# A cross-attention and feed-forward kernel: the 4-byte matmuls of a pair of heads in one group, and the first blocks re-ordered

## The chip, the cores and the metric

The kernel runs on one core of a Trainium2 chip. The metric is the device time of one execution in microseconds. TensorE (PE) does the matmuls, VectorE (DVE), ScalarE (ACT) and GpSimd (POOL) the elementwise work, and SyncE (SP) issues every DMA.

## The reference

There are 16 sequences of 64 tokens (T = 1024 tokens), width 512, 32 heads of 128. Cut to what matters:

```python
q = layernorm(x) @ Wq;  k = ctx @ Wk;  v = ctx @ Wv        # 1024 x 4096 each
score = q @ k.T / sqrt(128) + position_bias                # by sequence and head, 64 x 64
probs = softmax(where(mask, score, -inf))
x = x + (probs @ v) @ Wo
y = layernorm(x)
x = x + y @ base_W.T + base_b + 2 * lora(y)                # router of 8 experts, rank 16
```

All is float32. The large products are made of fp32r parts ("hi" and "lo"), three matmuls for each; the scores, the transpositions and the products with v are plain 4-byte matmuls.

## The kernel before

**Blocks.** v, k and q are made in 48 blocks of two heads (or of 128+128 tokens for v): blocks 0 to 15 are v, 16 to 31 k, 32 to 47 q (`QA` = 32). A block is a 2x2 product by Strassen's way in Winograd's form: seven products p of half size, each of 6 matmuls of 512 columns (`times(n, p)`, line 1253 inside `product`). Products 1, 6, 5, 3 of a block add up in one PSUM bank, 2, 7, 4 in another. Between them ACT copies the bank out (`copy_p1` after 1, `copy_u` after 6, `copy_v` after 5, `copy_c12` after 3), and DVE makes the quarters `c11` (after 2), `c22` (after 7), `c21` (after 4). Product 6 waits for `c1_made` (the copy after 1), 7 for `c11_made`, 5 for `u_made`, 3 for `v_made`, 4 for `c22_made`. Block 0 is made by the plain eight products, so that it can start before sums of its operand exist.

**Weights.** A block of k or q has its own weight set w of seven slots: three are parts of the loaded `wk_raw`, four are sums that POOL makes (`sums_of_b`, tile `twk`). ACT casts a slot to "hi" (`higher(w, slot)`) once the product of the block before that used it is done, DVE subtracts for "lo" (`lower_w`). v has four sets, each for four blocks.

**Pairs.** A pair i of heads 2i, 2i+1 needs q (block 32+i, one tile q, written over in each block), and k and v, which earlier blocks stored in HBM (`load_k`, `load_v`, single buffers). For each head h: `scores(h)` (32 matmuls of 64 columns into bank `pS`), DVE adds the bias, takes the row's largest off (lines 1069, 1073, 1075), ACT makes the exponential, DVE the weights (1082 to 1088), `turn_p(h)` transposes them (4 matmuls, line 1418), ACT copies them to pT, `times_v(h)` (64 matmuls of 64 columns, line 1433), ACT and DVE split the result into oT (`o_high`, `o_low`). `times_wo(i, t)` multiplies oT by Wo for token tile t (6 matmuls of 512 columns into bank `pY[t % 2]`), and DVE adds it to y (`add_tile`, line 1063), which frees the bank for tile t+2. Wo comes with `load_wo`, ACT casts it (`wo_high`, line 746), POOL subtracts for "lo" (`lower_wo`, line 564). POOL also adds the mask to each loaded bias (`add_mask`, line 547).

**Order.** Each engine works through a list written out by hand, with semaphores between them. In a period of the pair stage (a block n of q with pair n-32 and the `times_wo` of the pair before) PE's list is: scores, 1, wo0, scores, 2, wo1, wo2, turn, 6, wo3, times_v, 7, wo4, turn, 5, wo5, times_v, 3, wo6, 4, wo7. Ahead of it stands the opening: ctx tiles are transposed (`turn_pair`), and for each tile j seven slots of operand A are made (`first_high`/`first_low`, `rows_out`, `sums_of_a`, `sums_high`/`sums_low`, `last_high`/`last_low`). Behind the pairs stands the feed-forward part, whose weights are transposed in `ffn_weights`.

## Time and profile before

| | |
|---|---|
| median of 3 runs | 833.14 us (831.48 to 834.26) |
| profiled execution | 832.47 us, span 830.7 us |
| PE busy | 803.3 us (97%) |
| DVE / ACT / POOL busy | 582.0 / 341.0 / 232.3 us |
| mean granted TensorE clock | 0.99 of full speed |
| chain that ended last | PE 88%, DVE 6%, ACT 2% |
| HBM read, written | 81.64 MB, 35.65 MB |

The columns of the trace's answers are told with each group of rows below. A matmul's duration overlaps the next one's, so lengths are best read from start to start. "Idle before" names what the engine waited for.

### The profile page before, as it was taken

The numbers are of one execution on the slowest core, as the hardware profiler recorded it, in microseconds if no ns is written. First come the engines' busy times: TensorE is split into PE (matmuls) and PEld (weight loads), VectorE is DVE, ScalarE is ACT, GpSimd is POOL, SyncE is SP. The second block draws the span as 40 slices with busy tenths as digits, with TensorE's granted clock in tenths as the row PEclk, the third lists the DMA queues.
The fourth block names the chain that finished last, engine by engine and source line by source line (L and its number), as shares of the span: only waits on it lengthen the run. The fifth ranks groups of instructions, "written<-read, shape, count | busy, mean of one in ns | idle before, by whom it ended". The sixth has DMA issues, their size and how long they took to land.

```text
span 830.7 us, 16317 instructions
## 1 busy us (share of the span) xinstructions
PE 803.3 (97%) x6366; PEld 652.7 (79%) x6366; DVE 582.0 (70%) x1023; ACT 341.0 (41%) x657; POOL 232.3 (28%) x227
## 2 busy tenths in 40 slices
PE   8689999999999999969999999999999999998998
PEld 6578888888888888758888878888887878886786
DVE  4674435347677665588788888788787888758872
ACT  4544435245565554444334433344334433333410
POOL 0050404113424333253133322333133322111340
PEclk9789999999999999999999999999999999999999
DMA  6335665334454546564553436443563435442002
GB/s 215 99 142 169 231 224 178 114 130 163 153 177 153 176 148 203 193 188 135 153 176 112 141 108 179 134 145 106 152 178 112 137 110 152 122 150 38 1 9 93
DMA packets 108075, 118.35 MB, mean 142 GB/s; under 512 B 44240, under 2 KB 77008, under 8 KB 107999
## 3 DMA queue, kind: packets, MB, share of 16 engines
q1 hardware_dynamic: 107998, 117.31, 44.9%
q8 instruction: 51, 0.84, 0.4%
q14 instruction: 26, 0.20, 0.1%
HBM read 81.64 MB, written 35.65 MB: 141 GB/s over the span
## 4 chain that ended last, share of the span: by engine, by line
PE 88%; DVE 6%; ACT 2%; issue 1%; DMA 1%; POOL 0%; SPq 0%; ACTq 0%; DVEq 0%; POOLq 0%
PE pP L1253 38%; PE pY L1253 37%; PE pO L1433 4%; PE pS L1408 4%; PE pO L1253 2%; PE pT_ L1418 2%; DMA wk_raw<-in_L_xattn_Wq 1%; ACT wv_hi L624 1%; DVE co_lo L843 1%; PE pS L1299 1%; DVE oT_lo L843 0%; PE pT_ L1299 0%; DVE wk_lo L843 0%; DVE sums_c L887 0%; PE pO L1299 0%
## 5 line engine op out<-in xcount | busy, mean ns | idle before, releaser
L1063 DVE TENSOR_TENSOR y<-y,pY 128x512 f32<-128x512 f32 x124 | 84.4, 681 | 41.2 <-PE pY L1253 41.0
L1253 PE MATMUL pY<-wo_hi,oT_hi 128*128 128x512 f32 x248 | 97.8, 394 | 2.4 <-DVE y L1063 2.4
L1253 PE MATMUL pP<-xo_hi,wk_hi 128*128 128x512 f32 x224 | 97.2, 434 | 2.6 <-DVE q L853 1.7
L843 DVE TENSOR_TENSOR wk_lo<-twk,wk_hi 128x256 fp32r<-128x256 f32 x128 | 80.8, 643 | 23.7 <-ACT wk_hi L624 23.7
L1253 PE MATMUL pY<-wo_lo,oT_hi 128*128 128x512 f32 x248 | 96.8, 390 | 0.0
L1253 PE MATMUL pY<-wo_hi,oT_lo 128*128 128x512 f32 x248 | 96.5, 389 | 0.0
L1253 PE MATMUL pP<-xo_lo,wk_hi 128*128 128x512 f32 x224 | 88.7, 396 | 0.0
L1253 PE MATMUL pP<-xo_hi,wk_lo 128*128 128x512 f32 x224 | 88.4, 394 | 0.0
L547 POOL TENSOR_TENSOR bias<-bias,madd 128x512 f32<-128x512 f32 x32 | 42.0, 1313 | 139.5 <-DMA bias<-in_fside_Bx32xSxS 139.5
L624 ACT CAST wk_hi<-twk 128x256 fp32r<-128x256 f32 x128 | 52.1, 408 | 56.2 <-PE pP L1253 45.3
L843 DVE TENSOR_TENSOR wk_lo<-wk_raw,wk_hi 128x256 fp32r<-128x256 f32 x96 | 53.1, 553 | 20.9 <-ACT wk_hi L624 20.7
L624 ACT CAST wk_hi<-wk_raw 128x256 fp32r<-128x256 f32 x96 | 39.1, 407 | 45.7 <-PE pP L1253 38.1
L1253 PEld LDWEIGHTS pY<-wo_hi,oT_hi 128*128 128x128 f32 x248 | 46.7, 188 | 12.9 <-DVE y L1063 3.1
L564 POOL TENSOR_TENSOR wo_lo<-wo_raw,wo_hi 128x1024 fp32r<-128x1024 f32 x16 | 38.7, 2418 | 61.9 <-ACT wo_hi L746 61.9
L541 POOL TENSOR_TENSOR twk<-wk_raw,twk 128x256 f32<-128x256 f32 x32 | 23.6, 738 | 114.2 <-DVE wk_lo L843 114.2
L1253 PEld LDWEIGHTS pY<-wo_lo,oT_hi 128*128 128x128 f32 x248 | 46.5, 188 | 10.2
L1253 PEld LDWEIGHTS pY<-wo_hi,oT_lo 128*128 128x128 f32 x248 | 46.6, 188 | 10.0
L739 ACT CAST oT_hi<-pO 128x512 fp32r<-128x512 f32 x64 | 34.4, 590 | 47.8 <-PE pO L1433 47.8
L1253 PEld LDWEIGHTS pP<-xo_hi,wk_hi 128*128 128x128 f32 x224 | 42.3, 189 | 13.2 <-issue 3.0
L1253 PEld LDWEIGHTS pP<-xo_lo,wk_hi 128*128 128x128 f32 x224 | 42.3, 189 | 9.6
L843 DVE TENSOR_TENSOR oT_lo<-pO,oT_hi 128x512 fp32r<-128x512 f32 x64 | 41.2, 686 | 10.3 <-ACT oT_hi L739 9.4
L530 POOL TENSOR_TENSOR twk<-wk_raw 128x256 f32<-128x256 f32 x32 | 24.5, 767 | 85.4 <-DVE wk_lo L843 57.0
(256 smaller groups left out, 1887.5 us busy)
## 6 DMA issues: line engine op xcount, KB each, us to landing
v_hbm<-stage SPq DMA_DIRECT2D x64, 256.0 KB, 2.3
k_hbm<-stage SPq DMA_DIRECT2D x64, 256.0 KB, 3.2
k<-k_hbm SPq DMA_DIRECT2D x16, 1024.0 KB, 5.3
v<-v_hbm SPq DMA_DIRECT2D x16, 1024.0 KB, 6.1
wk_raw<-in_L_xattn_Wk SPq DMA_DIRECT2D x16, 512.0 KB, 4.5
wo_raw<-in_L_xattn_Wo SPq DMA_DIRECT2D x16, 512.0 KB, 3.7
bias<-in_fside_Bx32xSxS SPq DMA_DIRECT2D x128, 64.0 KB, 2.7
wk_raw<-in_L_xattn_Wq SPq DMA_DIRECT2D x16, 512.0 KB, 4.3
```

Of the source, the lines that this page charges most:

```text
L530: nc.gpsimd.tensor_tensor(tw[:, 0, :, :], raw_block(w, 1, 1), raw_block(w, 0, 1), ALU.subtract).then_inc(tw_made, 1)
L541: nc.gpsimd.tensor_tensor(tw[:, 3, :, :], raw_block(w, 1, 0), tw[:, 1, :, :], ALU.subtract).then_inc(tw_made, 1)
L547: nc.gpsimd.tensor_tensor(b[:, :, :], b[:, :, :], madd[:, :, :], ALU.add).then_inc(bias_made, 1)
L564: nc.gpsimd.tensor_tensor(lo[:, :, :], wo_raw[:, :, :], hi[:, :, :].bitcast(F32), ALU.subtract).then_inc(wo_l, 1)
L624: nc.scalar.copy(w_part(w, 0)[:, slot, :, :], w_source(w, slot)).then_inc(w_hi[slot], 1)
L739: nc.scalar.copy(of_parity(oT[i % 2][0], s, n), pO[n][:, :].rearrange("p (t q) -> p t q", q=S)).then_inc(o_hi, 1)
L843: nc.vector.tensor_tensor(dst, src, hi.bitcast(F32), ALU.subtract).then_inc(done, 1)
L1063: nc.vector.tensor_tensor(y[:, t, :], y[:, t, :], src[:, :], ALU.add).then_inc(y_added, 1)
L1253: mm = nc.tensor.matmul(bank_, a, b, start=first and n == 0, stop=last and n == len(terms) - 1, skip_group_check=read_between)
L1408: mm = nc.tensor.matmul(pS[64 * half:64 * half + 64, blk * S:(blk + 1) * S], q[:, h % 2, b * S:(b + 1) * S], k[:, h % 2, b * S:(b + 1) * S ...
L1418: mm = nc.tensor.transpose(pT_[:, j * P:(j + 1) * P], pr[h % 2][:, 2 * j:2 * j + 2, :].rearrange("p a k -> p (a k)"), ident[:, :])
L1433: mm = nc.tensor.matmul(pO[i][64 * d:64 * d + 64, t * S:(t + 1) * S], v[rows, t, s * DH + 64 * d:s * DH + 64 * d + 64], pT[rows, t, :], st ...
```

## The change

PE's list in a pair period becomes: turn, turn, scores, scores, times_v, times_v, 1, 2, 6, 7, wo0, wo1, 5, wo2, wo3, 3, wo4, wo5, 4, wo6, wo7. Turn, times_v and wo are now of pair i, the scores of pair i+1, and the block is n = 34+i. So that this can be, pair 0's q is block 31 and the last k block is 32 (`Q0`); scores go to the `pY` banks, the second head's transposition and result to `pS` and `pT_`; pT, mx, sm, rs are double, oT is single, `sc` is gone (the scores are worked on in `pr`). DVE's softmax is cut into `biased`, `largest`, `less_max`, `add_up`, `weights`, and its list begins a period with six of these and four `o_low`. SP issues k(i+2) ahead of the two biases. POOL's list is the same. The last pair's part is re-ordered too, with A's and the router's weights ahead of the base weights.

In the opening ACT's copies of block 0's quarters are moved ahead of casts, block 2's products begin between those of block 1, and the sums of tile 0 are made in block 5 rather than 2; blocks 4 to 15 of v take the token tiles in the order 1, 2, 3, 0.

```diff
+Q0 = NV + NK - 1
 QA = NV + NK
+def block_of_q(m):
+
+    return QA + m if m else Q0
...
+def tokens_of(n):
+
+    return n if n < 4 else (n + 1) % 4
+ORDER = [(1, 1), (0, 2), (1, 2), (0, 4), (0, 3), (0, 7), (1, 6), (1, 7), (2, 1), (2, 2), (1, 5), (1, 3), (2, 6),
+         (2, 7), (1, 4), (2, 5)]
+for n_ in range(3, QA + 1):
     ORDER += [(n_, 1), (n_ - 1, 3), (n_, 2), (n_ - 1, 4), (n_, 6), (n_, 7), (n_, 5)]
-ORDER += [(QA, p) for p in (1, 2, 6, 7, 5)] + [(QA - 1, 3), (QA - 1, 4), (QA, 3), (QA, 4)]
+ORDER += [(QA, 3), (QA, 4)]
...
-        pW = [pP[0], pP[1], pP[0], pP[1], pP[0], pP[1], pS]
+        pW = [pP[0], pP[1], pP[0], pP[1], pP[0], pP[1], pP[0]]
+
+
+        pT_of = [pT_, pS]
+        pO_of = [pO, [pT_, pS]]
...
-            if n < QA:
-                return stage[n % 2][i][:, :]
-            return q[:, i % 2, i // 2 * HALF:(i // 2 + 1) * HALF]
+            if is_q(n):
+                return q[:, i % 2, i // 2 * HALF:(i // 2 + 1) * HALF]
+            return stage[n % 2][i][:, :]
...
+
                     for i in range(4):
-                        sp.wait_ge(put[0][i], 16 * QA // 2)
+                        sp.wait_ge(put[1][i], 16 * (Q0 // 2))
+                        sp.wait_ge(put[0][i], 16 * (NV // 2 + 1))
                     load_k(0)
...
-            for i in range(NP):
-                if i + 23 < NSET:
-                    load_wk(i + 23)
-                if i + 1 < NP:
-                    sp.wait_ge(s_read, 2 * i + 1)
-                    load_bias(2 * i + 2)
-                    sp.wait_ge(s_full, 2 * i + 2)
-                    load_k(i + 1)
-                    sp.wait_ge(s_read, 2 * i + 2)
-                    load_bias(2 * i + 3)
-                    sp.wait_ge(wo_l, i + 1)
-                    load_wo(i + 1)
-                    sp.wait_ge(o_full, 4 * (i + 1))
-                    load_v(i + 1)
-                if i == NP - 2:
+            for i in range(4):
+                sp.wait_ge(put[0][i], 16 * (QA // 2 + 1))
+            load_v(0)
+            for i in range(NP - 1):
+                sp.wait_ge(wo_l, i + 1)
+                load_wo(i + 1)
+                if i + 2 < NP:
+                    sp.wait_ge(s_full, 2 * i + 4)
+                    load_k(i + 2)
+                    for s in range(2):
+                        sp.wait_ge(s_read, 2 * i + 3 + s)
+                        load_bias(2 * i + 4 + s)
+                if i + 24 < NSET:
+                    load_wk(i + 24)
+                sp.wait_ge(o_full, 4 * (i + 1))
+                load_v(i + 1)
+                if i == NP - 4:
+
+                    sp.wait_ge(w_lo[5], NSET - 1)
+                    sp.wait_ge(tw_made, 4 * (NSET - 1))
...
+                if n == Q0 - 1:
+                    pool.wait_ge(mask_made, 1)
+                    add_mask(0)
+                    add_mask(1)
...
+            piece_of_first(1, 3, pP[0], c12_made)
             higher(0, 2)
-            piece_of_first(2, 4, pP[1], c21_made)
-            piece_of_first(1, 3, pP[0], c12_made)
             piece_of_first(3, 7, pP[1], c22_made)
+            first_high(2)
+            copy_u(1)
+            rows_out(2)
+            last_high(2)
             higher(0, 4)
-            for n in range(1, QA + 1):
+            copy_p1(2)
+            sums_high(2)
+            copy_v(1)
+            higher(0, 6)
+            copy_c12(1)
+            copy_u(2)
+            first_high(3)
+            rows_out(3)
+            last_high(3)
+            copy_v(2)
+            sums_high(3)
...
+                turned_p(h)
+                turned_p(h + 1)
+                o_high(h)
+                o_high(h + 1)
                 copy_p1(n)
+                exp(h + 2)
+                higher_of(w, 0)
+                exp(h + 3)
+                higher_of(w, 1)
                 copy_u(n)
-                if w is not None:
-                    higher(w, 2)
-                o_high(2 * i)
-                if w is not None:
-                    higher(w, 3)
-                wo_high(i)
-                turned_p(2 * i + 1)
+                higher_of(w, 2)
+                higher_of(w, 3)
+                wo_high(i + 1)
                 copy_v(n)
-                if w is not None:
-                    higher(w, 4)
-                o_high(2 * i + 1)
+                higher_of(w, 4)
                 copy_c12(n)
-                if w is not None:
-                    higher(w, 5)
...
+            sums_of_a(1)
             lower_w(0, 5)
+            sums_low(1)
             first_t3()
             first_t2()
-            sums_of_a(1)
-            sums_low(1)
+            lower_w(0, 3)
             lower_w(0, 2)
             make_c11(1)
-            lower_w(0, 3)
+            first_low(2)
             first_t1()
+            first_t4()
             lower_w(0, 4)
-            first_t4()
-            for n in range(1, QA + 1):
+            sums_of_a(2)
+            make_c11(2)
+            sums_low(2)
+            lower_w(0, 6)
+            make_c22(1)
+            sums_of_a(3)
+            make_c21(1)
+            make_c22(2)
+            sums_low(3)
+            for n in range(3, QA):
...
+                biased(h + 2)
+                largest(h + 2)
+                biased(h + 3)
+                less_max(h + 2)
+                largest(h + 3)
+                less_max(h + 3)
                 o_low(h, 0)
                 o_low(h, 1)
                 o_low(h + 1, 0)
                 o_low(h + 1, 1)
+                lower_of(w, 0)
+                make_c11(n)
+                lower_of(w, 1)
+                add_up(h + 2)
+                weights(h + 2)
+                lower_of(w, 2)
+                lower_of(w, 3)
+                add_tile(i, 0)
+                add_up(h + 3)
+                add_tile(i, 1)
+                weights(h + 3)
+                make_c22(n)
+                add_tile(i, 2)
+                lower_of(w, 4)
+                add_tile(i, 3)
+                lower_of(w, 5)
+                add_tile(i, 4)
+                add_tile(i, 5)
                 make_c21(n)
-                add_tile(i - 1, 7)
-                if w is not None:
-                    lower_w(w, 6)
+                add_tile(i, 6)
+                lower_of(w, 6)
+                add_tile(i, 7)
...
             turn_pair(2)
-            for p in (6, 7, 5):
-                times(1, p)
-            for n in range(2, QA):
+            times(1, 6)
+            times(1, 7)
+            times(2, 1)
+            times(2, 2)
+            times(1, 5)
+            times(1, 3)
+            times(2, 6)
+            turn_pair(3)
+            times(2, 7)
+            times(1, 4)
+            times(2, 5)
...
             def scores(h):
-                if h % 2 == 0:
-                    pe.wait_ge(ld_k, 16 * (h // 2 + 1))
-                    pe.wait_ge(c11_made, QA + h // 2 + 1)
+                m, s = h // 2, h % 2
+                n = block_of_q(m)
+                if s == 0:
+                    pe.wait_ge(ld_k, 16 * (m + 1))
+                pe.wait_ge(c12_made if s else c11_made, n + 1)
+
+                if m == 0:
+                    pe.wait_ge(c21_made if s else c12_made, Q0 + 1)
+                elif m == 1:
+                    pe.wait_ge(s_read, s + 1)
                 else:
-                    pe.wait_ge(c12_made, QA + h // 2 + 1)
-                if h >= 1:
-                    pe.wait_ge(s_read, h)
+                    pe.wait_ge(y_added, NT * (m - 1) - 1 + s)
...
-                    if pair * NT + t >= 2:
+                    if t < 2:
+
+                        pe.wait_ge(s_read, 2 * pair + 3 + t)
+                    else:
                         pe.wait_ge(y_added, pair * NT + t - 1)
                 dst = pL[t % 4] if pair == last_pair else pY[t % 2]
                 cols = slice(t * P, (t + 1) * P)
-                o, w = oT[pair % 2], wo[pair % 2]
+                o, w = oT, wo[pair % 2]
...
+            n = QA
+            times(n, 1)
+            times(n - 1, 3)
+            times(n, 2)
+            times(n - 1, 4)
+            times(n, 6)
+            scores(0)
+            scores(1)
+            for p in (7, 5, 3, 4):
+                times(n, p)
+            for p in (1, 2, 6, 7, 5, 3, 4):
+                times(n + 1, p)
...
+            for i in range(NP - 2):
+                n = QA + 2 + i
                 h = 2 * i
                 turn_p(h)
-                times(n, 6)
-                times_wo(i - 1, 3)
+                turn_p(h + 1)
+                scores(h + 2)
+                scores(h + 3)
                 times_v(h)
-                times(n, 7)
-                times_wo(i - 1, 4)
-                turn_p(h + 1)
+                times_v(h + 1)
+                for p in (1, 2, 6, 7):
+                    times(n, p)
+                times_wo(i, 0)
+                times_wo(i, 1)
                 times(n, 5)
-                times_wo(i - 1, 5)
-                times_v(h + 1)
+                times_wo(i, 2)
+                times_wo(i, 3)
                 times(n, 3)
-                times_wo(i - 1, 6)
+                times_wo(i, 4)
+                times_wo(i, 5)
                 times(n, 4)
-                times_wo(i - 1, 7)
-            h = 2 * last_pair
-            scores(h)
-            times_wo(last_pair - 1, 0)
-            times_wo(last_pair - 1, 1)
-            scores(h + 1)
-            times_wo(last_pair - 1, 2)
-            times_wo(last_pair - 1, 3)
+                times_wo(i, 6)
+                times_wo(i, 7)
...
             turn_p(h)
-            times_wo(last_pair - 1, 4)
+            turn_p(h + 1)
+            scores(h + 2)
+            times_v(h)
+            times_v(h + 1)
+            scores(h + 3)
             ffn_weights(0)
-            times_v(h)
             ffn_weights(1)
-            times_wo(last_pair - 1, 5)
-            turn_p(h + 1)
-            times_wo(last_pair - 1, 6)
+            for t in range(4):
+                times_wo(i, t)
             ffn_weights(2)
             ffn_weights(3)
-            times_wo(last_pair - 1, 7)
-            times_v(h + 1)
-            for n in range(DC, NFW):
-                ffn_weights(n)
+            times_wo(i, 4)
+            times_wo(i, 5)
+            ffn_weights(4)
+            times_wo(i, 6)
+            times_wo(i, 7)
+            turn_p(h + 2)
+            turn_p(h + 3)
+            ffn_weights(5)
+            times_v(h + 2)
+            times_v(h + 3)
+            ffn_weights(6)
...
```

## Rows read from the trace of the kernel before

**Rows 1.** Page: busy time of an engine (share of the span), instructions.
```profile
PE 803.3 (97%) x6366; PEld 652.7 (79%) x6366; DVE 582.0 (70%) x1023; ACT 341.0 (41%) x657; POOL 232.3 (28%) x227
```
**Rows 2.** Waits of PE: who waited for whom, us in total, times, longest.
```profile
PE pP L1253 <- ACT stage L654: 5.0, 1, 5.0
...
PE pP L1253 <- DVE stage L859: 2.2, 1, 2.2
PE pY L1253 <- ACT v_s L609: 1.9, 1, 1.9
```
**Rows 3.** Windows: stretch, length, busy time by engine, granted clock, DMA share, GB/s.
```profile
20.00:30.00 10.00, 5.04 (x14) 3.71 (x13) 7.41 (x11) 3.91 (x5) 0.00 (x0) 0.66 0.00 0
...
38.90:44.00 5.10, 5.10 (x15) 4.02 (x16) 1.90 (x3) 0.92 (x2) 0.00 (x0) 0.67 1.00 321
...
347.00:370.00 23.00, 17.12 (x259) 12.91 (x258) 18.18 (x29) 10.29 (x21) 11.34 (x12) 1.00 0.61 177
...
749.00:757.00 8.00, 5.61 (x52) 4.24 (x53) 7.69 (x11) 1.91 (x3) 2.38 (x1) 1.00 0.35 37
```
**Rows 4.** Timeline of PE (start, duration): product 6 of block 3.
```profile
59.65 0.63 PE L1253 MATMUL pY<-wv_hi,co_hi 128*128 128x512 f32 x1
```
**Rows 5.** Timeline of DVE in the opening.
```profile
17.86 1.22 DVE L952 TENSOR_TENSOR twv<-wv_raw 128x1024 f32<-128x1024 f32 x1
```
**Rows 6.** Timeline of PE in a pair period: scores, transposition, next period.
```profile
562.10 0.39 PE L1253 MATMUL pY<-wo_lo,oT_hi 128*128 128x512 f32 x1
562.41 1.15 PE L1408 MATMUL pS<-k,q 128*64 128x64 f32 x32
563.50 0.50 PE L1253 MATMUL pP<-xo_hi,wk_hi 128*128 128x512 f32 x1
563.83 0.39 PE L1253 MATMUL pP<-xo_hi,wk_lo 128*128 128x512 f32 x1
...
567.71 0.60 PE L1418 MATMUL pT_<-ident,pr 128*128 128x128 f32 x4
568.07 0.48 PE L1253 MATMUL pP<-xo_hi,wk_hi 128*128 128x512 f32 x1
568.38 0.40 PE L1253 MATMUL pP<-xo_hi,wk_lo 128*128 128x512 f32 x1
...
589.05 1.15 PE L1408 MATMUL pS<-k,q 128*64 128x64 f32 x32
```
**Rows 7.** Timeline of PE in the last pair: transpositions, then times_v.
```profile
757.64 0.60 PE L1470 MATMUL pP<-ident,bw_raw 128*128 128x128 f32 x4
758.17 1.16 PE L1433 MATMUL pO<-pT,v 64*64 64x64 f32 x64
```
**Rows 8.** Timeline of DVE in a pair period.
```profile
564.98 0.69 DVE L1069 SCALAR_TENSOR_TENSOR sc<-pS,bias 128x512 f32<-128x512 f32 x1
...
566.42 0.69 DVE L1075 TENSOR_TENSOR sc<-sc,mx 128x512 f32<-128x512 f32 x1
567.03 0.69 DVE L853 TENSOR_TENSOR q<-pP,c_s 128x512 f32<-128x512 f32 x1
...
572.85 1.29 DVE L843 TENSOR_TENSOR oT_lo<-pO,oT_hi 128x512 fp32r<-128x512 f32 x2 [0.45 <-ACT oT_hi L739]
...
575.77 2.50 DVE L843 TENSOR_TENSOR wk_lo<-twk,wk_hi 128x256 fp32r<-128x256 f32 x2
```
**Rows 9.** Timeline of ACT (first line) and of POOL in the same period.
```profile
574.12 1.05 ACT L746 CAST wo_hi<-wo_raw 128x1024 fp32r<-128x1024 f32 x1
...
570.23 1.29 POOL L547 TENSOR_TENSOR bias<-bias,madd 128x512 f32<-128x512 f32 x1 [4.13 <-DMA bias<-in_fside_Bx32xSxS]
575.24 2.41 POOL L564 TENSOR_TENSOR wo_lo<-wo_raw,wo_hi 128x1024 fp32r<-128x1024 f32 x1 [3.73 <-ACT wo_hi L746]
```
**Rows 10.** Timeline of SP's DMA issues in the same period.
```profile
563.61 0.37 SPq L410 DMA_DIRECT2D k<-k_hbm  x1
565.69 2.57 SPq L403 DMA_DIRECT2D bias<-in_fside_Bx32xSxS  x4
```

501 lines of the change are left out of this document (243 added, 258 removed).

## The prediction

> **What bounds the kernel now.** I read the page's busy times first: PE is busy for 803.3 of 830.7 us [rows 1], so only 27 us of idle time can be given back at all, beside what PE does slowly. The list of PE's waits says where that idle time lies: none in the steady stretches, 9.1 us in three waits of the opening [rows 2], and, by the windows, 5.9 us where the pair stage begins [rows 3] (23.00 less 17.12). The windows also show work at the lower clock level behind long waits: a mean granted clock of 0.66 and 0.67, that is about half of each stretch at 1.2 GHz [rows 3]. Then I read the timeline of one pair period, 26.64 us long (562.41 to 589.05) [rows 6]; 13 whole periods are like it. It has no idle time but has joints. From the last wide matmul before the scores to the second one behind them pass 1.73 us (562.10 to 563.83) [rows 6]. Two wide matmuls take 0.455 of that, and 32 score matmuls take 0.96 (1.15 less the last one's 0.22, over 31 starts: 0.030 each). So 0.32 is the price of going in and out, 0.33 with what the next few starts are late. The same sum for a transposition (567.71 to 568.38, 0.67) leaves 0.01 [rows 6]: it is free. A period has four groups with joints, two of scores and two of times_v.
>
> **The joints.** Before: 64 groups of 0.34 and 32 transpositions of 0.02, 22.5 us. After: 14 groups of turn, turn, scores, scores, times_v, times_v, one of two score groups, and about three in the last pair. Going from transpositions into a 4-byte matmul does cost: 758.17 less 757.64 is 0.53 for four transpositions of 0.108 [rows 7], so 0.09; coming out costs 0.25. The trace has no step from scores to times_v. Its price lies between 0 and what a whole way out and in costs, 0.28; I take 0.1, as both sides of it are 4-byte matmuls. Left are 14 x 0.45 and about 0.9, 7.2 in all: the joints give 15.3 (12.6 to 16.9). The Trainium skill, TensorEngine Tiling (Array Packing), Key Properties, says that a change of the tiling mode drains TensorE. By that rule scores (128 rows by 64 columns) to times_v (64 by 64) pays in full, and the joints would give 12.7.
>
> **The opening.** Three waits of 5.0, 2.2 and 1.9 [rows 2], and behind them the clock: PE's 5.04 busy us at 0.66 cost 1.7, 5.10 at 0.67 cost 1.7 [rows 3], a third stretch counted at 1.6. That is 14.1 that could go before 59.65, where product 6 of block 3 starts [rows 4]. The largest goes surely: ACT copies C21 before the casts that now stand ahead of it. What is late next: the "lo" part of slot 2. DVE has to do sums_low(1), first_t3, first_t2, and slots 3 and 2, at about 1.14 each (1.22 less the overlap) [rows 5]; they end near 25.0, and PE is there at 24.0: 1.1. Then product 3 of block 1 waits for `v_made`, because ACT makes sums_high(2) first: 1.3. Then the v weights of set 1 land 6 us sooner, and POOL's four sums fall on DVE's work for blocks 3 and 4: 0.8. I take 14.1 less 3.3, so 10.8 (7 to 13).
>
> **Where the pairs begin.** 5.9 us of idle time in 347 to 370, a further 1.9 behind it with a slow stretch, and restarts, about 9.2. In the new order block 32 and 33 run without a pair's work between 5 and 3, and PE waits for copy_v each time: about 0.6 for the copy (wo_high, twice as wide, takes 1.05 [rows 9]), and 0.4 for the matmul's tail and the two signals, 1.0. Two of these: 7.2 saved (5 to 8.5). Pair 0's scores have a product each ahead of them, and v's load has 13 us. **The last pair**: PE is busy 5.61 of 8.00 us [rows 3]; the new list waits again for o_low before wo0 and for add_tile before wo2 and wo3. I take 1.4 saved (1 lost to 3 saved).
>
> So far: 832.5 (the profiled execution, 0.7 under the median of the three) - 15.3 - 10.8 - 7.2 - 1.4 = **797.8** if no new wait came. In a pair period that is 25.65 for 26.64. Moving the copies to other banks and the double pT cost nothing: same instructions, same durations. SP's list has k ahead of the biases, which matters below.
>
> **What the new order makes wait.** Let PE's first transposition of a period be time 0. The scores begin at 0.96, the first head's are done at 2.11. DVE then has in its queue, ahead of c11: biased, largest (dependent steps 0.72 each: 564.98 to 566.42 is two) [rows 8], biased 0.60, less_max 0.61, largest 0.72, less_max 0.61, four o_low of 0.60 (the row of two is 1.29), a 256-column lower 0.34, c11 0.69. From 2.16 these give o_low from 6.03, the lower at 8.43, c11 from 8.77 to 9.46. PE comes to product 7 at 9.15 and, with 0.14 for the signal (an estimate), starts it at 9.60: **0.45 lost, and 0.09 for the restart**. That much is sure.
>
> Behind it, wo2 needs add_tile 0, which stands in DVE's queue behind lower 2 and 3. Both of their inputs are in SBUF, and the timeline shows what POOL does to such an instruction: `wo_lo` runs from 575.24 for 2.41 [rows 9], and the two lowers that began at 575.77 took 2.50 together instead of 0.76 [rows 8]; the add, the o_low and the bias step, with an input in PSUM, are not held. In the new order ACT's cast of slot 3 waits for product 7 (done at 11.2), then comes wo_high (1.05, [rows 9]), and POOL's wo_lo asks at 12.67. Without POOL, DVE would have done lower 3 at 12.28, 0.4 us sooner. But POOL also has two masks of 1.29 [rows 9] in this stretch. k is issued at 3.13, the first four bias loads from 3.56, and their mask would start 4.5 us later (565.69 to 570.23) [rows 9, 10], at 8.1; k's megabyte now goes just ahead of them, so I put it at 9.6. The second one is at 10.9 to 11.1 by its issues. They hold the product of rs and `some` at 10.67, and then the weights, until 13.2. wo_lo comes in behind these and holds lower 2 until 15.6; lower 3, and add_tile 0 from 16.15 to 16.83; wo2 starts at 16.97 instead of 15.14: **1.8 lost**. add_tile 1 has add_up between, 1.2 more, and a POOL sum in the way: wo3 **0.45 lost**. With the restarts that is 2.85 in a period (2.4 to 3.3), 13 periods, 37 (the 14th has no weight set). The Trainium skill, SBUF — State Buffer, Who interferes with whom, states it as a rule: a DVE instruction with two SBUF inputs and a GpSimd one that reads SBUF exclude each other for the whole instruction. The trace agrees (2.50 for 0.76).
>
> A wait of 1.8 is near those behind which the clock fell (1.9, 2.2) and near 749 to 757, with 2.39 idle in two parts and a clock of 1.00 [rows 2, 3]. One fall costs 1.7. I count two in 13 periods, 3 us (0 to 12).
>
> **Forecast**: 797.8 + 37.0 + 3 = **838**. Its own range is 826 to 850.
>
> **Rivals.** *A: only product 7 waits.* If wo_lo finds lower 3 done, the 1.8 and 0.45 fall away. That needs the masks to cost DVE under 0.4 us between 8.43 and 12.67, or to land so early that the first (8.1) stands before the lower at 8.43 and delays c11: then product 7 starts at 10.4 to 10.6, everything behind shifts, and lower 3 just beats wo_lo. The period is 26.1 in the first form, 27.1 in the second: 797.8 + 13 x 0.45 = 804 to 797.8 + 13 x 1.4 = 816. For it: the margins are 0.3 to 0.4 us, less than the spread of a load; bias landings without k ahead speak for the second form. Against it: both masks must run in this stretch. This is the case on the other side, faster, and it decides at lower 3 ending before POOL asks.
> *B: a mixture.* Loads vary by some tenths from period to period, so that some periods are 27 and others 28.5: 816 to 828.
> *C: the joints aren't saved.* If a group of scores or times_v paid its 0.34 even next to its like, only the transpositions' places would change: 15.3 falls to about 0, and with A's waits the time is 819 to 831, with the forecast's 853. The 32 matmuls inside a group run at 0.030 with no joint between them, so I hold it for unlikely.
>
> **How the numbers follow.** Forecast 0.50, A 0.27, B 0.16, C 0.07. 0.3%, about what a measurement of this kernel can tell from no change, is 2.5 us, 830.6 to 835.6. Of the forecast 0.38 is slower, 0.07 within, 0.05 faster; A and B are faster; C is spread over all three. Together: faster 0.50, same 0.09, slower 0.41. The range goes from A's lower form to the forecast with four falls of the clock: 803 to 847; about 0.1 is left out on each side.
>
> **What would show it.** Right: the first wide matmul behind times_v 0.15 after its last; period 28.1 to 28.8; product 7 waiting for DVE's q, wo2 for DVE's y, each 13 times; a lower of 2.4 or more beside each wo_lo; PE idle of 0.5, 1.8 and 0.4 in a period; nothing left of the 5.0. Wrong: a period under 27, or a lower 3 that ends before wo_lo starts, makes the time A's; a clock under 1.00 in most periods makes it more than 847; product 3 of block 1 waiting over 3 us would undo the opening's part.

## The result, and the profile after

The changed kernel takes **830.24 us** (median of 20 runs, 820.92 to 835.47), the kernel before 833.39 in the same rounds (20 runs, 829.98 to 836.57): a ratio of 0.9948, interval 0.9928 to 0.9967. It is half a per cent faster. Five of the 20 runs, the ones from 833.5 up, are slow ones, over 1.5% above the fastest; the ratio is taken from the other 15, whose median is 829.67. The forecast was 838.0 with a range of 803 to 847: the time lies in the range, and the sign is the other one.

The profiled execution of the changed kernel took 832.8 us, with a span of 831.0 us. That is 2.6 above its median; the kernel before was profiled 0.9 under its own. All accounts below are of profiled executions, so they must explain +0.3 us and not -3.

The page's busy times, which answer to [rows 1]:

```profile
PE 794.6 (96%) x6366; PEld 651.9 (78%) x6366; DVE 589.9 (71%) x1023; ACT 335.6 (40%) x657; POOL 240.2 (29%) x227
```

PE is busy for 8.7 us less, and the span is 0.3 longer: idle time has been added. The list of PE's waits says where (who waited for whom: us in total, times, longest us):

```profile
PE pY L1361 <- DVE y L1106: 16.7, 12, 1.9
PE pS L1548 <- issue: 1.6, 2, 1.2
...
PE pP L1361 <- DVE q L905: 1.5, 8, 0.2
PE pY L1361 <- ACT v_s L642: 1.3, 1, 1.3
...
PE pT_ L1548 <- issue: 0.8, 2, 0.5
PE pY L1361 <- DVE wv_lo L895: 0.7, 1, 0.7
```

The first line is `add_tile` ahead of `times_wo`: the wait that the forecast put there. Of [rows 2], the waits of 5.0 and 2.2 are gone; in the opening 1.3 for `v_s` and 0.7 for a lower part of v's weights are left, both at places where the forecast put one. "issue" marks a wait that nothing in the profile released; the last section comes back to it. The windows (stretch, length, busy us of PE, PEld, DVE, ACT, POOL, granted clock, DMA share, GB/s) show the opening, one whole period with that wait, a place where the clock fell behind it, and a period without it:

```profile
20.00:30.00 10.00, 9.27 (x45) 7.47 (x45) 9.20 (x10) 6.27 (x10) 0.00 (x0) 1.00 0.14 35
...
489.65:518.33 28.68, 26.43 (x291) 21.42 (x290) 23.46 (x36) 9.81 (x20) 8.45 (x8) 1.00 0.46 129
564.00:568.00 4.00, 3.81 (x10) 2.99 (x11) 3.93 (x9) 0.00 (x0) 1.14 (x2) 0.57 0.48 132
576.84:603.87 27.03, 26.21 (x291) 21.42 (x290) 21.82 (x36) 9.81 (x20) 8.72 (x8) 1.00 0.47 138
```

The stretch 20 to 30 held 5.04 busy us at a clock of 0.66 [rows 3]; it now holds 9.27 at 1.00. The 13 periods with a weight set are between 27.03 and 29.96 us long, 28.28 on the mean, where one of before took 26.64 [rows 6].

Inside the period from 489.65, first PE, then DVE, then POOL (start, us, engine, line, operation, out<-in, shape, count, idle time before it and who ended it; PE's lines that are left out are marked):

```profile
489.65 0.60 PE L1533 MATMUL pT_<-ident,pr 128*128 128x128 f32 x4
...
490.62 2.08 PE L1523 MATMUL pY<-k,q 128*64 128x64 f32 x64
492.63 1.16 PE L1548 MATMUL pO<-pT,v 64*64 64x64 f32 x64
...
499.22 0.47 PE L1361 MATMUL pP<-xo_hi,wk_hi 128*128 128x512 f32 x1 [0.19 <-DVE q L905]
...
506.85 0.50 PE L1361 MATMUL pY<-wo_hi,oT_hi 128*128 128x512 f32 x1 [1.94 <-DVE y L1106]
```
```profile
500.48 1.79 DVE L1145 TENSOR_TENSOR pr<-pr,rs 128x512 f32<-128x512 f32 x1
502.18 4.02 DVE L895 TENSOR_TENSOR wk_lo<-twk,wk_hi 128x256 fp32r<-128x256 f32 x2
506.12 0.67 DVE L1106 TENSOR_TENSOR y<-y,pY 128x512 f32<-128x512 f32 x1
```
```profile
500.42 2.99 POOL L579 TENSOR_TENSOR bias<-bias,madd 128x512 f32<-128x512 f32 x2 [10.09 <-DMA bias<-in_fside_Bx32xSxS]
503.37 2.55 POOL L597 TENSOR_TENSOR wo_lo<-wo_raw,wo_hi 128x1024 fp32r<-128x1024 f32 x1
```

To read it: the weights (L1145) take 1.79 beside POOL's first mask, where they take 0.69 alone; the two lowers take 4.02 instead of 0.76, the first beside the second mask, the second beside `wo_lo`; `add_tile` stands behind them, and PE waits 1.94 for it. Product 7 starts 9.57 behind the period's start (forecast 9.60), wo2 at 17.20 (forecast 16.97).

In the period from 576.84 the two lowers take their turns with the masks, one behind each (1.52 and 1.51 long), both are over when `wo_lo` runs, and wo2 doesn't wait; wo3 does, 0.63:

```profile
587.67 0.69 DVE L1145 TENSOR_TENSOR pr<-pr,rs 128x512 f32<-128x512 f32 x1
588.28 2.95 DVE L895 TENSOR_TENSOR wk_lo<-twk,wk_hi 128x256 fp32r<-128x256 f32 x2
```
```profile
587.94 3.00 POOL L579 TENSOR_TENSOR bias<-bias,madd 128x512 f32<-128x512 f32 x2 [10.42 <-DMA bias<-in_fside_Bx32xSxS]
590.91 2.58 POOL L597 TENSOR_TENSOR wo_lo<-wo_raw,wo_hi 128x1024 fp32r<-128x1024 f32 x1
```

Of the 13 periods, three have no held lower of 2.6 (27.0 to 27.3 long). In the one of 27.3 PE itself had stopped for 1.22 in times_v, so that all of DVE's and POOL's work met otherwise. In the other ten a lower is held for 2.6: the one of slot 2 in six, the one of slot 3 in four.

### The profile page after: what moved, and what is told of

Same layout as the page of the kernel before. It is cut to its first block, busy times and chain, and to the rows that moved or that the text cites. A ratio compares the mean times of both kernels' runs of the same rounds, so it can differ in the third digit from the quotient of the medians.

```text
span 831.0 us, 16334 instructions
## 1 busy us (share of the span) xinstructions
PE 794.6 (96%) x6366; PEld 651.9 (78%) x6366; DVE 589.9 (71%) x1023; ACT 335.6 (40%) x657; POOL 240.2 (29%) x227
## 4 chain that ended last, share of the span: by engine, by line
PE 70%; DVE 24%; issue 3%; ACT 2%; DMA 1%; POOL 0%; SPq 0%; ACTq 0%; DVEq 0%; POOLq 0%
PE pY L1361 32%; PE pP L1361 28%; DVE wk_lo L895 5%; DVE oT_lo L895 3%; PE pY L1523 3%; DVE pr L1145 2%; DVE y L1106 2%; PE pO L1361 2%; DVE pr L1114 2%; DVE sm L1136 2%; DVE pr L1128 2%; DVE rs L1140 2%; DVE q L905 1%; DVE mx L1123 1%; PE pT_ L1533 1%
## 5 line engine op out<-in xcount | busy, mean ns | idle before, releaser
L1361 PE MATMUL pY<-wo_hi,oT_hi 128*128 128x512 f32 x248 | 100.9, 407 | 18.0 <-DVE y L1106 16.7
L1361 PE MATMUL pP<-xo_hi,wk_hi 128*128 128x512 f32 x210 | 84.6, 403 | 2.3 <-DVE q L905 1.5
L1361 PE MATMUL pP<-xo_hi,wk_lo 128*128 128x512 f32 x210 | 82.1, 391 | 0.3 <-issue 0.3
L1361 PE MATMUL pP<-xo_lo,wk_hi 128*128 128x512 f32 x210 | 82.0, 390 | 0.0
L895 DVE TENSOR_TENSOR wk_lo<-wk_raw,wk_hi 128x256 fp32r<-128x256 f32 x96 | 46.2, 482 | 32.4 <-ACT wk_hi L657 32.1
L1361 PE MATMUL pP<-co_hi,wk_hi 128*128 128x512 f32 x126 | 49.4, 392 | 0.8 <-ACT v_s L642 0.8
L597 POOL TENSOR_TENSOR wo_lo<-wo_raw,wo_hi 128x1024 fp32r<-128x1024 f32 x16 | 41.8, 2610 | 25.8 <-ACT wo_hi L781 25.8
L1361 PE MATMUL pP<-co_lo,wk_hi 128*128 128x512 f32 x126 | 49.1, 390 | 0.0
L1361 PE MATMUL pP<-co_hi,wk_lo 128*128 128x512 f32 x126 | 49.0, 389 | 0.0
L1361 PE MATMUL pY<-wv_hi,co_hi 128*128 128x512 f32 x112 | 44.0, 392 | 2.3 <-ACT v_s L642 1.3
```

Of the source, the lines that this page charges most:

```text
L597: nc.gpsimd.tensor_tensor(lo[:, :, :], wo_raw[:, :, :], hi[:, :, :].bitcast(F32), ALU.subtract).then_inc(wo_l, 1)
L895: nc.vector.tensor_tensor(dst, src, hi.bitcast(F32), ALU.subtract).then_inc(done, 1)
L1361: mm = nc.tensor.matmul(bank_, a, b, start=first and n == 0, stop=last and n == len(terms) - 1, skip_group_check=read_between)
```

## The experiments

The theory, called L: POOL's `wo_lo`, brought up by the masks, holds a lower of DVE for its whole length, and `add_tile` 0 and PE's wo2 behind it; this is what ate the joints. Its rivals: DVE has simply too much to do ahead of `add_tile` 0 (D); the masks alone are the cause (M). A ratio is that to the kernel before on the same chip, with its 95% interval behind it; a time is the median of 4 to 12 runs. The names e1 to e12 are those by which the expectations call the runs.

### wo_lo made by DVE, late in the period (e1)

```diff
-                lower_wo(i)              # POOL, behind the masks
...
+                lower_wo(i + 1)          # DVE, behind add_tile(i, 5)
```

(Cut; the first and the last `lower_wo` move to DVE's list too.)

> The changed kernel with one thing different: the lower part of the next output weight (wo_lo, 1024 columns, 2.6 us on POOL) is made by DVE, behind add_tile 5 of the pair, where DVE has idle time, and no longer by POOL. DVE gets about 1.2 us more work in a period (a lower of 256 columns takes 0.41, of 512 0.69), POOL 2.6 less. Theory L (POOL's wo_lo holds DVE's lower of slot 3, and add_tile 0 and wo2 behind it): the lowers of 2.61 are gone in all periods, wo2's wait (mean 1.30 of 13 periods in the changed kernel) goes to under 0.2, the period from 28.28 to 26.7 to 27.0, the time from 830 to 808 to 816. Rival D (DVE simply has too many operations ahead of add_tile 0): nothing ahead of add_tile 0 is fewer, so the wait of wo2 stays at 1.3 and the time is 829 to 835. Rival M (the two masks alone are the cause): the masks are still there, so the wait stays as under D.

Measured: 810.64, ratio 0.9748 (0.9723 to 0.9772). Of the 16.7 us of PE's waits for DVE's y one wait of 0.48 is left, in a period in which a mask holds the lower of slot 2 for 1.51. Twelve periods are 26.0 to 26.9 long; the first is 29.0, with a stop of 1.54 that nothing released and a wait of 0.93 for product 7's c11. D falls: DVE has more work, and the wait is all but gone. M falls as the whole cause: the masks are where they were, and alone they cost that 0.48.

### add_tile 0 and 1 ahead of the lower of slot 3 (e2)

```diff
                 lower_of(w, 2)
-                lower_of(w, 3)
                 add_tile(i, 0)
-                add_up(h + 3)
                 add_tile(i, 1)
+                lower_of(w, 3)
+                add_up(h + 3)
```

> The changed kernel with add_tile 0 and add_tile 1 ahead of the lower of slot 3 in DVE's list of each pair; nothing is added or left out. Theory L: the held lower (2.61) is still there in most periods, but nothing that PE needs in this period stands behind it but add_up and add_tile 2; wo2's wait goes from a mean of 1.30 to under 0.2 and the period from 28.28 to about 26.9, 809 to 818 in all. Rival D (DVE is late by its sum of work): the order gives add_tile 0 0.4 us at most, the time is 824 to 831. Rival T (the next wait takes its place: add_up, weights and c22 come later by the held lower and product 4, or the next pair's transposition, waits for them): 822 to 830.

Measured: 822.0, ratio 0.9862 (0.983 to 0.9894), a miss by 4 us.

```profile
PE pY L1361 <- DVE y L1106: 11.0, 10, 1.6
```

This expectation took the lower of slot 3 for the one that is held. In six periods it is the lower of slot 2 (2.60 long), which still stands ahead of `add_tile` 0, and in exactly six periods of this kernel wo2 waits, 0.7 to 1.6 by idle time. In four others the wait has moved on to wo4, 0.4 to 1.2, because add_tile 2 now stands behind the lower of slot 3, add_up and the weights, of which at least one is held. That is rival T of the expectation, with its 822. The miss agrees with L, corrects its place, and shows T beside it.

### wo_lo ahead of the masks (e3)

```diff
+                lower_wo(i)
                 add_mask(2 * i + 2)
                 add_mask(2 * i + 3)
-                lower_wo(i)
```

(Cut; in the first round of POOL's loop the masks stay ahead.)

> The changed kernel with POOL's wo_lo ahead of the two masks of a pair in POOL's list. wo_lo then asks as soon as ACT's wo_high is done, about 12.3 us behind the period's first transposition, and the masks run behind it, from about 14.9. Theory L with the masks' share as I put it in the prediction (the masks hold the weights and the lower of slot 2 by 1.1 each and so bring lower 3 into wo_lo): without them DVE ends lower 3 at 12.2 to 12.6, a narrow race; where it is won the period is 26.9, where it is lost wo_lo ends at 14.9, add_tile 0 at 15.6 and wo2 waits 0.6 instead of 1.7: 812 to 821 in all. Rival W (wo_lo alone holds lower 3, the masks have no share): lower 3 is still caught for 2.6 and ends near 15, the wait of wo2 is 1.0 or more in most periods: 824 to 830.

Measured: **807.08**, ratio 0.9708 (0.9686 to 0.973), better than either bound. DVE, then POOL, in the period from 457.47:

```profile
468.29 0.69 DVE L1148 TENSOR_TENSOR pr<-pr,rs 128x512 f32<-128x512 f32 x1
468.90 0.75 DVE L898 TENSOR_TENSOR wk_lo<-twk,wk_hi 128x256 fp32r<-128x256 f32 x2
```
```profile
470.13 2.40 POOL L597 TENSOR_TENSOR wo_lo<-wo_raw,wo_hi 128x1024 fp32r<-128x1024 f32 x1 [11.98 <-ACT wo_hi L784]
```

Without masks ahead of them the weights take 0.69, the lowers are over at 469.65, and `wo_lo` begins 0.5 us later, in all 13 periods. Most periods are 26.0 long. So the masks' share was as the prediction had it: they bring the lowers into `wo_lo`. The work is the same, only its order on POOL is not.

### c11 ahead of the fourth o_low (e5)

```diff
                 o_low(h + 1, 0)
+                make_c11(n)
                 o_low(h + 1, 1)
                 lower_of(w, 0)
-                make_c11(n)
```

This run and e6 are made on the kernel of e3.

> The kernel of e3 (wo_lo ahead of the masks on POOL) with c11 ahead of the fourth o_low and of the lower of slot 0 in DVE's list of each pair. My step in the prediction: product 7 waits because c11 stands behind four o_low and a lower, 0.45 (0.35 in the traces, in two of three periods). With c11 from 8.1 to 8.8 behind the first transposition and PE there at 9.2, the 0.35 goes in all periods and wo0, which needs the fourth o_low by 10.5, does not wait: period 26.0 to 25.65, 802 to 804 for e3's 807. Rival: PE's wait moves on to wo0 or to product 1 of the next block, because the sum of DVE's work is what counts: 806 to 808.

Measured: 802.11, ratio 0.9625 (0.96 to 0.9651).

```profile
454.29:479.84 25.55, 25.55 (x291) 21.66 (x290) 20.41 (x36) 9.80 (x20) 8.62 (x8) 1.00 0.50 146
```

This is a period without any wait, in a window as above: 25.55, where the prediction had 25.65. Eight of 13 are like it; in the other five, three periods apart, PE stops inside the group with nothing that released it.

### Scores and times_v in two groups (e6), and the same with wo_lo on DVE (e10)

```diff
                 scores(h + 3)
+                times(n, 1)
+                times(n, 2)
                 times_v(h)
                 times_v(h + 1)
-                for p in (1, 2, 6, 7):
+                for p in (6, 7):
```

With it ACT's copy after product 1 comes ahead of `o_high`, and `c11` ahead of the `o_low`s.

> The kernel of e3 with the pair's group of 4-byte matmuls cut in two: products 1 and 2 stand between the scores and times_v, and c11 and the copy for it come ahead of the o parts. It measures a joint by itself. By my sum one way out of the 4-byte matmuls and in again costs 0.25 and 0.09, 0.34, and the step from scores to times_v inside a group 0.1: so joints of 0.35 a period become 0.58 to 0.69, the wait of product 7 goes, and the period is 25.75 to 26.0, 804 to 808. If joints cost nothing next to their like only by accident (rival C: every group of scores or times_v pays wherever it stands), the joints would not change: period 25.65, 802 to 804. A second matter: five of 13 periods of e3 have a wait of 0.3 to 1.4 in the middle of times_v that no engine or load released; if it comes from the number of small matmuls that follow each other without a pause, it should be gone or smaller here.

Measured: **839.35**, ratio 1.0079 (1.0051 to 1.0106): 37 us more than e5, and against all that was expected. PE's waits, then DVE and POOL in the period from 493.84, which repeats 13 times within 0.04 us:

```profile
PE pY L1364 <- DVE y L1109: 29.3, 26, 1.5
```
```profile
506.82 2.94 DVE L898 TENSOR_TENSOR wk_lo<-twk,wk_hi 128x256 fp32r<-128x256 f32 x2
```
```profile
506.81 2.67 POOL L597 TENSOR_TENSOR wo_lo<-wo_raw,wo_hi 128x1024 fp32r<-128x1024 f32 x1 [12.30 <-ACT wo_hi L784]
```

Here the masks come behind `wo_lo`, and still the lower of slot 3 is held for 2.60, because `wo_lo` begins together with the lower of slot 2. In e5 it stood the other way round by little: the lowers ran at 491.53 for 0.75, and `wo_lo` began at 492.06. A few tenths of a microsecond in when DVE arrives decide 3 us of a period. The same cut, with `wo_lo` made by DVE as in e1 (POOL has only sums and masks):

> The kernel of e6 (scores and times_v of a pair in two groups) with the lower part of the output weight made by DVE behind add_tile 5 as in e1, so that POOL has only sums and masks. In e6 the lower of slot 3 stood 2.60 us in all 13 periods, beside a wo_lo that began 0.35 us ahead of it, and PE waited 1.67 and 0.91. Theory L: those 2.6 us a period, 34 in all, are the lock alone, and the cut of the group costs one way out and in again, 0.20 by the joints of e6 against e5 (0.11 and 0.09 more): period 25.8 to 26.1, 804 to 809. Rival: the order of the products is what made PE wait (DVE behind products 6 and 7): PE still waits 1 us or more for DVE's y, 815 or above.

Measured: 812.83, ratio 0.9752 (0.9726 to 0.9779), twelve periods of 26.3 to 26.9 and a first one of 27.4. So 26.5 of the 37 us went with `wo_lo`'s place alone. I had expected 4 us less: the masks start at 9.3 to 12.4 here and hold a lower of slot 0 or 1 (up to 1.31 for 0.42) and the product of rs and `some` (up to 1.09 for 0.17), and wo2 starts up to 0.55 late and wo3 about 0.3. The joints are in both traces as expected: the cut costs 0.20 more than the direct step from scores to times_v, by the first wide matmul behind the scores and the start of times_v behind the last one (0.34 and 0.32 instead of 0.23). The lines are of e6:

```profile
496.81 0.50 PE L1364 MATMUL pP<-xo_hi,wk_hi 128*128 128x512 f32 x1
497.15 0.40 PE L1364 MATMUL pP<-xo_hi,wk_lo 128*128 128x512 f32 x1
...
499.46 0.39 PE L1364 MATMUL pP<-xo_lo,wk_hi 128*128 128x512 f32 x1
499.78 1.16 PE L1551 MATMUL pO<-pT,v 64*64 64x64 f32 x64
```

The expectation's second matter came out too: neither e6 nor e10 has a stop in the group that nothing released.

### The bias loads ahead of k (e8)

In SP's list of a pair the two waits on `s_read` with their `load_bias` come ahead of `load_k`, in the changed kernel.

> The changed kernel with the two bias loads of a pair ahead of the load of k in SP's list, nothing else. It tests where the masks run and what that does. In the changed kernel the first mask starts at 10.3 on the mean behind the first transposition, the second at 11.6. With k behind them they should start near 8.2 and 9.7 and be over by 11. Theory L with rival A's second form from the prediction: the first mask holds the lower of slot 0, c11 is late by up to 1.1 and product 7 waits 0.5 to 1.4; wo_lo comes at 12.3 to 12.7 and lower 3 is ended near 12.5 or caught: period 27.0 to 28.3, 814 to 829, a mixture. If the masks' time had no share, the time would be the changed kernel's 829 to 832.

Measured: 816.6, ratio 0.9804 (0.9769 to 0.9839), inside the expected 814 to 829.

```profile
PE pP L1361 <- DVE q L905: 7.6, 10, 1.3
PE pY L1361 <- DVE y L1106: 1.6, 2, 0.9
```

The first mask starts 7.2 to 8.4 behind the period's start. In most periods it holds the lower of slot 0 (0.99 for 0.42 at 410.16, beside a mask from 409.58), product 7 waits for c11, everything behind shifts, and in 11 of 13 periods the lowers get past `wo_lo`; in the other two the lower of slot 3 is held for 2.6. The 11 are rival A in its second form, with periods of 26.1 to 27.1 where it had 27.1 throughout.

### The opening: C21's copy alone (e4), and with the sums ahead (e7)

Both are the kernel before, with a change in the opening alone. First ACT's list:

```diff
             sums_high(1)
+            piece_of_first(2, 4, pP[1], c21_made)
             higher(0, 3)
             higher(0, 2)
-            piece_of_first(2, 4, pP[1], c21_made)
```

> The kernel before with only ACT's copy of C21 of block 0 moved ahead of the casts of slots 3 and 2; the blocks' order, the pair stage and all else are as before. My step in the prediction: the wait of 5.0 us goes, with the 1.7 that the clock cost behind it, and the lower part of slot 2 is late next, by 1.1 and something for the copy of 0.6 that now stands ahead of the casts: 4 to 6 us are gained, 827 to 829. Rival: the casts of slots 3 and 2 are what PE really lacks, the wait only changes its name: under 2 us gained, 831 to 833. The waits of 2.2 and 1.9 should stay in either case.

Measured: 831.75, ratio 0.9995 (0.9979 to 1.0012): no gain. PE's waits, then ACT:

```profile
PE pP L1253 <- DVE stage L859: 3.3, 1, 3.3
PE pP L1253 <- ACT stage L654: 3.1, 1, 3.1
```
```profile
23.39 1.05 ACT L649 CAST co_hi<-sums_c 128x1024 fp32r<-128x1024 f32 x1 [4.17 <-DVE sums_c L896]
24.34 0.58 ACT L654 COPY stage<-pP 128x512 f32<-128x512 f32 x1
```

The copy of C21 stands directly behind `sums_high(1)`, and that cast waits 4.17 us for DVE, whose list has `first_t3` and `first_t2` ahead of the sums of tile 1. So the 5.0 of [rows 2] became 3.1 and the 2.2 became 3.3. The next run moves, besides, `sums_of_a(1)` and `sums_low(1)` ahead of `first_t3` and `first_t2` on DVE, and ACT's `higher(0, 5)` behind the copies, as the changed kernel has them.

> The kernel before with two moves in the opening: ACT's copy of C21 ahead of the casts of slots 3 and 2, as in the run that moved it alone, and on DVE the sums of tile 1 (four additions and their lower) ahead of twv t3 and t2, with ACT's cast of slot 5 behind the copies. In the run with the copy alone it still ended late, because ACT's list has the sums' cast ahead of it, which waits for DVE's sums behind t3 and t2 (2.5 us). Theory: with both moves the wait of 5.0 goes as a whole; the lower parts of slots 2 and 3 come no later than before, so product 3 of block 0 starts at 21 instead of 25.3 and 3 to 5 us are left at the end of the opening: 828 to 830.5. Rival: the waits of 2.2 and 1.9 grow by what the first one loses (they wait for DVE's and ACT's next steps, which have not moved): under 1 us gained, 831.5 to 833.5; then the opening's 11.8 us come from block 2 begun in block 1.

Measured: 829.95, ratio 0.9969 (0.995 to 0.9988), 2.6 us by the ratio. In the trace the transpositions of block 18 begin at 199.29, 3.5 us sooner than in the kernel before (202.82). The wait of 5.0 is gone, with one of 0.55 for a lower part behind it, and the one of 1.9 is 0.5; but these are left:

```profile
PE pP L1253 <- DVE stage L859: 3.3, 1, 3.3
PE pY L1253 <- ACT u_s L603: 2.4, 1, 2.4
```

PE arrives earlier at the next results of ACT and DVE, which come no earlier: the time is in the theory's range (828 to 830.5), but the rival holds in kind, with the 2.2 grown to 3.3 and a new wait of 2.4 for `u_s`. The two share the outcome. The changed kernel's opening gained 11.8 us by the same mark. What is left beyond these two moves, some 8, came with the rest of the new opening, above all the products of block 2 between those of block 1; no run has that part alone, so its cause is argued and not shown.

### The last pairs (e9, e11, e12)

The changed kernel waits in the stretch from 742.38 to 777.86 as well. DVE, POOL and PE there:

```profile
753.51 2.48 DVE L1145 TENSOR_TENSOR pr<-pr,rs 128x512 f32<-128x512 f32 x1
```
```profile
753.04 2.40 POOL L597 TENSOR_TENSOR wo_lo<-wo_raw,wo_hi 128x1024 fp32r<-128x1024 f32 x1 [21.01 <-ACT wo_hi L781]
```
```profile
757.01 0.66 PE L1594 MATMUL pP<-ident,bw_raw 128*128 128x128 f32 x4 [1.27 <-DVE ar_lo L895]
```

Again `wo_lo` holds an instruction, now the weights, and the split of a weight part behind it is late. Three ways out of it were tried on the kernel of e5. In DVE's list:

```diff
             add_tile(i, 0)
+            split_ffn(1)
             add_up(h + 2)
             add_tile(i, 1)
-            weights(h + 2)
             add_tile(i, 2)
-            split_ffn(1)
+            weights(h + 2)
```

> The kernel of e5 with DVE's list of the last pair but one changed: the lower part of the second a/router weight (split_ffn 1, its input in PSUM) comes right behind add_tile 0, and add_tile 2 ahead of the weights of head 28, which wo_lo on POOL holds for 2.47 there. In the changed kernel and in e5 PE waits 1.4 and 0.8 for these parts in the stretch in which my prediction saw 1.4 us of gain. Theory: the held weights are the cause here too; with nothing that PE needs behind them the 1.4 goes and most of the 0.8: 1.2 to 2 us off e5, 800 to 801.5. Rival: the next steps of DVE (the weights of the next head, the last parts of the weights) are late by as much and the waits move to the transposition or to the last split: within 0.5 of e5's 802.1.

Measured: 805.71 (801.56 to 809.12, 6 runs), ratio 0.9668 (0.9643 to 0.9693), no better than e5. In the trace, which is of the fastest of the six, the stretch between the last two groups of transpositions is 22.84 long for e5's 21.90. DVE, POOL, PE:

```profile
721.01 2.22 DVE L1143 TENSOR_TENSOR rs<-rs,some 128x8 f32<-128x8 f32 x1
```
```profile
720.86 2.35 POOL L597 TENSOR_TENSOR wo_lo<-wo_raw,wo_hi 128x1024 fp32r<-128x1024 f32 x1 [20.28 <-ACT wo_hi L784]
```
```profile
723.88 0.50 PE L1364 MATMUL pY<-wo_hi,oT_hi 128*128 128x512 f32 x1 [2.39 <-DVE y L1109]
```

An instruction of eight columns, 0.17 us of work, is held for 2.22. With ACT's `wo_high` one split later instead:

> The kernel of e5 with ACT's wo_high of the last pair behind the split of the third weight part, so that POOL's wo_lo asks about 4 us later, when the weights of head 28 are long done. In e5 wo_lo holds these weights for 2.47 in the last pair but one, and PE waits 1.4 and 0.8 behind; in e9, where only DVE's order was changed, wo_lo held the product of rs and some instead (0.17 us of work, 2.22 long) and add_tile 1 behind it, and PE waited 2.56 for that. Theory: with wo_lo out of the way both waits go nearly as a whole: 1.3 to 2 us off e5's 802.1, 800 to 801. Rival (DVE's sum of work ends late whatever POOL does): the waits stay within 0.4 and the time is 801.5 to 802.5.

Measured: 802.8, ratio 0.9643 (0.9624 to 0.9662): no gain over e5. `wo_lo` began at 726.27, and the weights of the next head, at 727.08, took 2.11; PE waited 2.03 for the split of a weight part behind them, and the granted clock was 0.93 in the stretch, which is 23.42 long. And last, the one `wo_lo` of the last pair made by DVE behind `add_tile(i, 7)`:

> The kernel of e5 with the lower part of the last output weight alone made by DVE, behind add_tile 7 of the last pair but one; the fourteen others stay on POOL. In e9 and e11 wo_lo held another instruction with two operands in SBUF as soon as the first was moved away from it (rs times some for 2.22, the weights of head 29 for 2.11), and nothing was gained. In e1 and e10, where POOL makes no wo_lo, this stretch, from the transpositions of the last pair but one to those of the last, is 20.40 us long for 21.9. Theory: it is 20.4 here too, 1.5 us off e5, 800 to 801.5. Rival: the 20.4 of e1 and e10 comes from something else in their lists, and DVE's 1.1 us more end in a later transposition of the last pair: 802 or above.

Measured: **800.43**, ratio 0.9598 (0.9574 to 0.9622). The stretch in a window of e5 (first line) and of this kernel:

```profile
711.73:733.63 21.90, 20.03 (x270) 15.92 (x269) 18.73 (x31) 7.77 (x14) 2.39 (x1) 1.00 0.45 120
```
```profile
713.86:734.30 20.44, 19.82 (x270) 15.93 (x268) 17.03 (x31) 7.68 (x14) 0.00 (x0) 1.00 0.49 133
```

It is 1.46 shorter, about as in e1 and e10 (20.40 long), and this is the fastest kernel of the study by its median, 4.0% under the kernel before. The interval of its ratio overlaps that of e5, so it is the stretch and not the time that shows the gain.

## Why the prediction was right and wrong

By stretches of the two profiled executions, with the start of the same PE work as marks:

| | forecast | measured |
|---|---|---|
| opening (to the transpositions of block 18, at 202.82 before and 191.00 after) | -10.8 | -11.8 |
| where the pairs begin | -7.2 | -9.2 |
| joints | -15.3 | -15.4 |
| new waits, 13 periods and the 14th | +37.0 | +32.7 |
| clock | +3 | +3.4 |
| last pair | -1.4 | +0.4 |
| sum | +5.3 | +0.1 |

Each measured entry is the time of a stretch less what PE's matmuls need there at their bare pitches (90 wide ones of 0.2273 in a period, transpositions of 0.108, small ones of 0.0297 and 0.015), compared between the two kernels; the spans differ by 0.3, and the 0.2 between is rounding. From the mark at 202.82 and 191.00 to the feed-forward part (777.55 and 777.86) the changed kernel takes 12.1 us longer (forecast 16.1).

**The joints**: right. A period of before has 1.50 us beyond PE's bare pitches, the period of 25.55 in e5 has 0.40: 1.10 saved, 15.4 in 14. The group has 0.09 on the way in, 0.11 to 0.12 from scores to times_v (490.62 to 492.63 less 64 x 0.0297) and 0.13 out, with 0.1 on the second wide matmul. The step from scores to times_v, for which I took 0.1 between 0 and 0.28, paid 0.12 and some 0.07 on its first starts. Rival C falls. By the Trainium skill, TensorEngine Tiling (Array Packing), Key Properties, a change of the tiling mode drains TensorE. The trace has 0.19 at most for this step, less than the 0.28 that I took for a full price.

**The new waits** (37.0 in the prediction): the mechanism was right, two terms were mis-sized. Product 7 starts at 9.57 for 9.60. `wo_lo` takes hold as described, but in 10 of 13 periods; wo2 starts 1.30 us late on the mean of the 13 and 1.7 where it occurs, which is the 1.8 of the prediction. The step that failed is "13 periods": I treated as sure for each period what stood on 0.4 us. From start to start, wo2's waits are 16.9 us for the 23.4 of the sum (13 x 1.8), and product 7's, of which I wrote "that much is sure", 2.8 for 5.9 (8 x 0.35 for 13 x 0.45). The measured 32.7 holds, besides, some 4 us of stops inside the group that nothing released, of which the prediction had none; without them the term is 28.7 for 37.0, so the table's agreement is in part luck. The first mask starts between 9.4 and 11.1, the second between 10.8 and 12.8 (10.2 and 11.7 on the mean; I had 9.6 and 11), so some lowers pass. Rival B, a mixture, was the right form, with the share of the forecast's kind larger than half; I gave it 0.16, and its 816 to 828 ends below the measured time. With ten such periods instead of 13 the forecast would have been 838 less 3 x 1.4 = 834, within what I called no change.

**The sign** turned on small terms: 3 x 1.4 from the periods that escape, 1.0 and 2.0 in the opening and where the pairs begin, 1.8 the other way in the last pair, and 2.6 by which the profiled execution lies above its median. The 20 runs span 14.6 us where before they span 6.6. Periods of two kinds 1.4 apart, and falls of the clock of 1.7 each (two in this trace: 0.57 over 564 to 568, behind a wait of 1.89), are of this size. The runs with a mean clock of 1.000 took 820.9 to 829.7, the three at 0.996 took 830.8 to 832.8.

**The opening**: the size was right, the reason given for its largest part was not enough. Two of the waits that were forecast to come next did come, 0.73 for 1.1 and 1.32 for 1.3; none was seen for the 0.8 of POOL's sums. But "The largest goes surely: ACT copies C21 before the casts" didn't hold by itself: that move alone gained nothing, since the copy's place in ACT's list is behind a cast that waits for DVE. I had read who waited (PE for ACT's copy) and not what ACT itself had waited for; [rows 5] shows DVE's `first_t3` in just this place.

**Where the pairs begin**: the two waits for `copy_v` came, 0.77 of idle time each for 1.0. Why the rest gained 2.0 more than forecast was not taken apart.

**The last pair**: wrong. I looked for waits of wo0, wo2 and wo3 there, and none came; but POOL's `wo_lo` runs in that stretch too, and I had not set it beside DVE's list. It costs 1.5 us, by e12, of the 1.8 between forecast and measurement.

**What would show it**: period 28.1 to 28.8: 28.28 on the mean. Product 7's wait 13 times: 8 times; in the others PE was late itself. wo2 waiting for DVE's y 13 times: 10 times. A lower of 2.4 or more beside each `wo_lo`: 10 of 13.

The held lowers are nothing new. The lines of before, of the changed kernel and of e5 (out<-in, shape, count, busy in all, mean ns):

```profile
L843 DVE TENSOR_TENSOR wk_lo<-twk,wk_hi 128x256 fp32r<-128x256 f32 x128 | 80.8, 643 | 23.7 <-ACT wk_hi L624 23.7
```
```profile
L895 DVE TENSOR_TENSOR wk_lo<-twk,wk_hi 128x256 fp32r<-128x256 f32 x128 | 81.7, 651 | 22.0 <-ACT wk_hi L657 22.0
```
```profile
L898 DVE TENSOR_TENSOR wk_lo<-twk,wk_hi 128x256 fp32r<-128x256 f32 x128 | 55.1, 443 | 22.0 <-ACT wk_hi L660 22.0
```

Before and after they are busy for 26 us more than in e5, where `wo_lo` holds none of them. That cost next to nothing before, where PE waits for DVE's y only twice, in the last pair (2.4 us), and 16.7 us of waits for DVE's y once `add_tile` 0 stood close behind.

## What to carry to other kernels

When a new order takes slack away, look for instructions that are already longer than their kind (here 2.5 for 0.76): what they cost was hidden, and comes out. Give a GpSimd instruction a time when the other engine has nothing with two SBUF operands to do, or give its work to that engine; moving single instructions away from it only changes which one is caught. And where the answer hangs on a margin of a few tenths, count periods as a mixture, and don't multiply one period by 13.
